# One transfer instead of two for the broadcast rows of a state-space scan

## The chip, the cores and the metric

The kernel runs on one core of a Trainium2 chip. The metric is device time in microseconds (us) of one launch. The core's engines run instruction streams of their own, each strictly in order, and meet only at semaphores: TensorE (PE, matrix products and transposes), VectorE (DVE, among others the scan), ScalarE (ACT, activation functions), GpSimd (POOL, elementwise products here) and SyncE (SP), which does nothing but issue transfers (DMAs) between DRAM and SBUF, the on-chip memory.

## The reference

The input is x of shape 32 x 512 x 256: 32 batches of 512 tokens of 256 features. Each batch goes through a modulated layer norm, causal attention of 16 heads beside a selective state-space layer, a feed-forward layer, and a routed low-rank layer. What the change touches is the state-space recurrence, with 512 inner channels and 16 states n for each:

```python
def step(h, inp):
    xt, dtt, Bt, Ct = inp
    h = jnp.exp(dtt[..., None] * A) * h + (xt * dtt)[..., None] * Bt[:, None, :]
    y = jnp.einsum('bn,bdn->bd', Ct, h)
    return (h, y)
```

B and C are, for each batch, 16 rows of 512 tokens each. They are the same for all channels. Everything is float32 here.

## The kernel before

The 512 channels lie on 128 partitions in four blocks. A scan is one channel block and one state n over all 512 tokens, so a batch has 64 scans, e = 0 to 63. Two scans (two channel blocks, the same n) make a unit, k = 0 to 31, with k = e // 2. A unit goes through these steps:

- SP broadcasts row n of B and row n of C from DRAM (`bc_d`) to all 128 partitions, each into its half of slot k mod 4 of the tile `bc` (function `bc_row`, steps rb_k and rc_k of SP's order, line 438).
- POOL writes the scan inputs of both scans, u times B's row, into two of the eight places of the ring `state` (`fill_states`, step fill_k, L584). It waits for B's row and for the PE sums that last read these two places, of the scans 2k-8 and 2k-7.
- ACT writes the decays into one of two PSUM banks (step dec_e, L708).
- DVE scans (step scan_e, L1201).
- The state is multiplied by C's row: on DVE (step c_e, L1209), or, in every fourth unit (k mod 4 = 3), on POOL (step pc_e, L571). This is the first reader of C's row.
- PE adds the product to the output sums in PSUM (step add_e, L940, four transposing matmuls).

B's half of a slot is free when fill_(k-4) is done (semaphore `b_ok`). C's half is free when the last product of unit k-4 is done, scan 2k-7 (`p_ok` for DVE, `pp_ok` for POOL). SP waits for that before it issues the transfer, and all that stands behind it in SP's order waits as well. Each half of each slot has a semaphore of its own for the landing.

What every engine does in which order is written out by hand in the table `ORDER`, one string for each engine, one turn for each batch. The names of a turn are played again for the next batch; "+" in front means the next batch and "-" the batch before. The turns of batches 2 to 29 are a loop of two turns. Between the scan steps stand the steps of the other layers: in SP's order `xr` (the input again for the residual, and gates, L504 to L510), `put` (the output, L513), `mt` (the row of maxima of the attention, L494), `ld` (q and k for the attention, L481 to L488), `qk` (q and k to DRAM, L458). In SP's order the rc steps do not stand in the order of k: rc11 stands behind rc12, rc13, rc14 and xr; rc19 behind rc20, rc21 and put; rc9 behind rc10; rc6 behind rc8; rc29 behind rc30. The matching rb steps stand far earlier.

## Time and profile before

| | us |
|---|---|
| median of 3 runs | 5942.51 |
| lowest, highest | 5938.76, 5949.41 |
| profiled execution, span | 5938.9 |
| PE busy | 5262.0 (89%) |
| DVE busy | 5103.3 (86%) |
| POOL busy | 4194.8 (71%) |
| ACT busy | 4094.7 (69%) |

The profiled execution is one run; its own time is given by its span, from the first to the last instruction, and it lies within the times of the runs. A share of busy time is a mean over stages that have different limits, so the question at each place is which wait ends last there. "SPq" is SP's queue of issues; the time from an issue to its landing is given apart. The unit of the batch and the number of the scan are not in the trace; they follow from the count of the instructions of a line in the order of the table. The rows below are of two successive batches, called batch 16 and batch 17 by this count (the first is batch 0).

### The profile page before, as it was taken

To read this page: it belongs to the slowest core of one execution; us is meant where nothing else is said; L and a number is where in the kernel's file an instruction comes from. 1 tells how busy PE (TensorE), PEld (TensorE's weight loads), DVE (VectorE), ACT (ScalarE), POOL (GpSimd) and SP (SyncE) were. 2 spreads that over 40 slices of the span, in tenths; PEclk is the share of its full clock that TensorE was granted. 3 is DMA by queue.
4 is the path that set the end of the run, shared out by engine and by line. 5 is a ranking of instruction groups with operands and counts; after the bars stand their busy time and mean duration, and the time that the engine had idled before them with its cause. 6 is when DMAs were issued, how large, how long until landed. Compare 5 with 4: busy or idle time off the path is not lost. (4 is left out here: it accounts for less than half of the span.)

```text
span 5938.9 us, 115651 instructions
## 1 busy us (share of the span) xinstructions
PE 5262.0 (89%) x32280; PEld 3518.1 (59%) x32280; DVE 5103.3 (86%) x7776; ACT 4094.7 (69%) x6407; POOL 4194.8 (71%) x2545
## 2 busy tenths in 40 slices
PE   4799989989898898989989899898988989899986
PEld 2466655656565566656566556565655666565664
DVE  3898889888899898998989898898998989989983
ACT  3677767767776766767767777677767667677763
POOL 3678767767677677776777677676776777767772
PEclk7899999999999999999999999999999999999997
DMA  4444444444454444454444444444444444444441
GB/s 129 132 140 142 140 148 149 142 128 142 135 152 147 129 142 128 144 152 135 143 126 140 144 151 143 127 141 133 152 148 126 142 133 143 151 142 137 142 129 39
DMA packets 521726, 814.74 MB, mean 137 GB/s; under 512 B 80432, under 2 KB 227288, under 8 KB 520976
## 3 DMA queue, kind: packets, MB, share of 16 engines
q1 hardware_dynamic: 513072, 805.79, 44.4%
q8 instruction: 296, 4.85, 0.3%
q14 instruction: 454, 3.72, 0.2%
q10 hardware_dynamic: 7904, 0.39, 0.1%
HBM read 716.50 MB, written 88.38 MB: 136 GB/s over the span
## 5 line engine op out<-in xcount | busy, mean ns | idle before, releaser
L584 POOL TENSOR_TENSOR state<-scan_in,bc 128x1024 f32<-128x1024 f32 x1024 | 2405.9, 2362 | 650.6 <-PE pY L940 504.2
L1201 DVE TENSOR_TENSOR_SCAN pD<-pD,state 128x512 f32<-128x512 f32 x1536 | 1851.2, 1216 | 190.1 <-ACT pD L708 119.9
L708 ACT ACTIVATE pD<-scan_in,A 128x512 f32<-128x512 f32 x2048 | 1397.5, 690 | 656.5 <-DVE state L1209 572.6
L940 PE MATMUL pY<-ident,state 128*128 128x128 f32 x8192 | 1214.0, 282 | 102.9 <-DVE state L1209 94.8
L940 PEld LDWEIGHTS pY<-ident,state 128*128 128x128 f32 x8192 | 928.6, 145 | 335.7 <-DVE state L1209 145.8
L1209 DVE TENSOR_TENSOR state<-pD,bc 128x512 f32<-128x512 f32 x1536 | 1024.6, 680 | 44.7 <-issue 24.6
L1259 DVE TENSOR_REDUCE mx<-pM 128x1 f32<-128x512 f32 (+3 forms) x1408 | 850.3, 630 | 69.8 <-PE pM L1030 67.5
L809 ACT ACTIVATE region<-pM 128x512 f32<-128x512 f32 (+1 forms) x1408 | 733.6, 556 | 255.3 <-PE pM L1048 224.8
L571 POOL TENSOR_TENSOR state<-state,bc 128x512 f32<-128x512 f32 x512 | 644.2, 1273 | 342.9 <-DVE state L1201 333.4
L1201 DVE TENSOR_TENSOR_SCAN state<-pD,state 128x512 f32<-128x512 f32 x512 | 606.0, 1207 | 105.0 <-ACT pD L708 105.0
L1046 PE MATMUL pM<-region 98*128 98x512 bf16 (+3 forms) x2048 | 535.5, 310 | 101.5 <-DMA region<-mrow 45.0
L1028 PE MATMUL pM<-region 96*128 96x512 bf16 (+3 forms) x2048 | 544.8, 314 | 79.2 <-DVE mx L1259 66.8
L1082 PE MATMUL pM<-region,w_f 128*128 128x512 f32 x1024 | 460.1, 600 | 18.1 <-ACT scan_in L846 14.2
L1091 PE MATMUL pM<-w_f,scan_in 128*128 128x256 f32 x2048 | 458.5, 383 | 5.7 <-ACT scan_in L850 5.7
L1091 PEld LDWEIGHTS pM<-w_f,scan_in 128*128 128x128 f32 x2048 | 387.9, 192 | 61.7 <-ACT scan_in L850 10.8
L1030 PE MATMUL pM<-mask_qk,identb 128*128 128x128 bf16 x2048 | 402.1, 225 | 0.0
L962 PE MATMUL pM<-region,vt 128*17 128x512 f32 (+3 forms) x4096 | 359.2, 439 | 46.2 <-ACT region L809 21.1
L1048 PE MATMUL pM<-identb,mask_qk 128*128 128x128 bf16 x2048 | 399.2, 223 | 0.0
L1046 PEld LDWEIGHTS pM<-region 98*128 98x128 bf16 x2048 | 204.1, 101 | 328.6 <-ACT region L809 143.0
L1015 PE MATMUL pM<-w_in,xnT 128*128 128x512 f32 x512 | 277.0, 668 | 96.0 <-issue 67.0
L1082 PEld LDWEIGHTS pM<-region,w_f 128*128 128x128 f32 x1024 | 189.5, 191 | 248.1 <-issue 210.5
L1028 PEld LDWEIGHTS pM<-region 96*128 96x128 bf16 x2048 | 205.8, 101 | 215.3 <-DVE mx L1259 121.0
(171 smaller groups left out, 8360.6 us busy)
## 6 DMA issues: line engine op xcount, KB each, us to landing
bc<-bc_d SPq DMA_DIRECT2D x2048, 256.0 KB, 4.0
region<-qk_d SPq DMA_DIRECT2D x640, 128.0 KB, 3.6
qk_d<-qkp SPq DMA_DIRECT2D x64, 384.0 KB, 2.6
qk_d<-ht SPq DMA_DIRECT2D x64, 384.0 KB, 3.1
xt<-in_x_dram SPq DMA_DIRECT2D x32, 512.0 KB, 5.7
hres_d<-xt SPq DMA_DIRECT2D x32, 512.0 KB, 5.1
region<-qk_d SPq DMA_DIRECT2D x256, 64.0 KB, 3.0
x<-hres_d SPq DMA_DIRECT2D x32, 512.0 KB, 5.9
```

What stands on the lines that cost most here:

```text
L571: nc.gpsimd.tensor_tensor(slot, slot, bc[:, e // JP % BC_SLOTS, 1, :], ALU.mult).then_inc(pp_ok.sem, 1)
L584: nc.gpsimd.tensor_tensor(state[:, at_:at_ + JP], us[:, parity(b), k // N * JP:(k // N + 1) * JP, :], bc[:, k % BC_SLOTS, 0, :].unsqueeze( ...
L708: act.activation(pD[DECAY_BANK[e]][:], dts[:, parity(b), j], ACT.Exp, scale=A[:, j, n:n + 1]).then_inc(a_ok.sem, 1)
L809: act.activation(probs[kb % 2][:, h:h + heads, 0:n], pM[bank_of(name)][:, 0:heads * n].rearrange("p (h t) -> p h t", h=heads), ACT.Exp, sc ...
L940: ins = pe.matmul(y_part(t, e % JP), state[:, e % RING, t * P:(t + 1) * P], ident[:], is_transpose=True, start=False, stop=(e % PASS >= PA ...
L1028: pe.matmul(ps[:, s * n:(s + 1) * n], q[0:QK_ROWS, h, qb * P:(qb + 1) * P], kk[0:QK_ROWS, h, 0:n], start=True, stop=False, skip_group_chec ...
L1046: pe.matmul(ps[:, i * n:(i + 1) * n], kk[0:QK_ROWS + 2, h + i, kb * P:(kb + 1) * P], q[0:QK_ROWS + 2, h + i, kb * P:L], start=True, stop=F ...
L1082: ins = pe.matmul(ps[:], w_f1[:, k, f * P:(f + 1) * P], h2T[:, k], start=(k == 0), stop=(k == KT - 1))
L1091: ins = pe.matmul(ps[:, t * D:(t + 1) * D], gT(b)[:, f, (2 * n + t) * P:(2 * n + t + 1) * P], w_f2[:, f, :], start=(f == 0), stop=(f == FT ...
L1201: v.tensor_tensor_scan(h if e in POOL_C else decay, decay, h, 0.0, ALU.mult, ALU.add)\
L1209: v.tensor_tensor(state[:, e % RING], pD[DECAY_BANK[e]][:], bc[:, slot, 1, :], ALU.mult)\
L1259: v.tensor_reduce(mx[:, g % 2].rearrange("p (h q) -> p h q", q=TB)[:, heads[0]:heads[-1] + 1, qb], pM[bank_of(name)][:, 0:len(heads) * n]. ...
```

## The change

B's and C's rows of a unit come with one transfer of 512 KB into both halves of the slot, with one semaphore. It is issued where C's row was issued, behind the wait for the last product of unit k-4. The rb steps go from SP's order; nothing else in any order is moved. POOL's fill and POOL's and DVE's products wait for the same semaphore.

```diff
--- before.py
+++ after.py
@@ -314,7 +314,7 @@
         dt_ps, dt_x, dt_e, dt_ok, u_ok = (sig("dt_ps", J), sig("dt_x", 2 * J), sig("dt_e", 2),
                                           sig("dt_ok", 1), sig("u_ok", 2))
         xd_ok, d_done = sig("xd_ok", J), sig("d_done", PASSES)
-        bc_in = [[sem(f"{row}_in{s}") for s in range(BC_SLOTS)] for row in "bc"]
+        bc_in = [sem(f"bc_in{s}") for s in range(BC_SLOTS)]
         a_ok, b_ok, s_ok, p_ok, y_ok = (sig("a_ok", SCANS), sig("b_ok", SCANS), sig("s_ok", SCANS),
                                         sig("p_ok", len(DVE_C)), sig("y_ok", SCANS))
         pp_ok = sig("pp_ok", len(POOL_C))
@@ -424,23 +424,19 @@
                 sp.dma_start(Ks[s][QK_ROWS:QK_ROWS + 2], ones_d).then_inc(ones_in, 16)
             sp.dma_start(mod_cols.rearrange("b p c -> p b c"), mod_t).then_inc(cols_stored, 16)
 
-            def bc_row(b, k, row):
+            def bc_rows(b, k):
 
                 slot = k % BC_SLOTS
 
                 before, last = (b, k - BC_SLOTS) if k >= BC_SLOTS else (b.next(-1), k - BC_SLOTS + UNITS)
                 if before.reg is not None or before.off >= 0:
-                    e = JP * last + JP - 1
-                    if row == 0:
-                        before.wait(sp, b_ok, e + 1)
-                    else:
-                        before.wait(sp, *product_after(e))
-                sp.dma_start(bc[:, slot, row], bc_d[b.index, k // N, row * N + k % N].partition_broadcast(P))\
-                  .then_inc(bc_in[row][slot], 16)
+                    before.wait(sp, *product_after(JP * last + JP - 1))
+                sp.dma_start(bc[:, slot], bc_d[b.index, k // N].rearrange("(r n) t -> n r t", r=2)[k % N]
+                             .partition_broadcast(P)).then_inc(bc_in[slot], 16)
 
             def step(name, b):
-                if name[:2] in ("rb", "rc"):
-                    bc_row(b, int(name[2:]), int(name[1] == "c"))
+                if name[:2] == "rc":
+                    bc_rows(b, int(name[2:]))
                 elif name == "load" and b.reg is None and b.off == 0:
                     pass
                 elif name == "load":
@@ -559,15 +555,15 @@
             def row(ap):
                 return ap.unsqueeze(1).broadcast_to([P, TB, D])
 
-            def row_in(b, k, row):
-
-                return Signal(bc_in[row][k % BC_SLOTS], 16 * UNITS // BC_SLOTS), 16 * (k // BC_SLOTS + 1)
+            def rows_in(b, k):
+
+                return Signal(bc_in[k % BC_SLOTS], 16 * UNITS // BC_SLOTS), 16 * (k // BC_SLOTS + 1)
 
             def times_c(b, e):
 
                 slot = state[:, e % RING]
                 b.wait(pool, s_ok, e + 1)
-                b.wait(pool, *row_in(b, e // JP, 1))
+                b.wait(pool, *rows_in(b, e // JP))
                 nc.gpsimd.tensor_tensor(slot, slot, bc[:, e // JP % BC_SLOTS, 1, :], ALU.mult).then_inc(pp_ok.sem, 1)
 
             def fill_states(b, k):
@@ -575,7 +571,7 @@
                 e, at_ = k * JP, k * JP % RING
                 if k == 0:
                     b.wait(pool, u_ok)
-                b.wait(pool, *row_in(b, k, 0))
+                b.wait(pool, *rows_in(b, k))
 
                 if e >= RING:
                     b.wait(pool, y_ok, e + JP - RING)
@@ -1205,7 +1201,7 @@
 
                 slot = e // JP % BC_SLOTS
                 b.wait(dve, s_ok, e + 1)
-                b.wait(dve, Signal(bc_in[1][slot], 16 * UNITS // BC_SLOTS), 16 * (e // JP // BC_SLOTS + 1))
+                b.wait(dve, Signal(bc_in[slot], 16 * UNITS // BC_SLOTS), 16 * (e // JP // BC_SLOTS + 1))
                 v.tensor_tensor(state[:, e % RING], pD[DECAY_BANK[e]][:], bc[:, slot, 1, :], ALU.mult)\
                  .then_inc(p_ok.sem, 1)
 
@@ -1362,10 +1358,9 @@
 
 ORDER = {engine: parse(text) for engine, text in {
     "SP": """
-        -rb22 -rb25 -rb23 -ld3 -rc23 -rb24 -mt2 -rc25 -rb26 -rc24 -rb27 -x1p -rc26 -rc28 -rb28 -rb29 -rc27 xp
-        -rb30 ld0 -mt3 -rb31 -rc30 -rc29 -rc31 +load rb1 rb0 rc0 rc1 rc2 rb2 rb3 rc3 rb4 ld2 rc4 rb5 rc5 rb7 rb6
-        rb8 rb9 rc8 rc6 rc7 ld1 rb10 rc10 rc9 rb11 rb12 rc12 rb13 rc13 rc14 -xr rc11 rc15 mt0 rb15 rc16 rb16 rb14
-        +qk0 +qk1 rb18 rc17 +qk2 rb20 rb17 rc18 +l1a rb19 mt1 rc20 rb21 +qk3 rc21 -put rc19 rc22
+        -ld3 -rc23 -mt2 -rc25 -rc24 -x1p -rc26 -rc28 -rc27 xp ld0 -mt3 -rc30 -rc29 -rc31 +load rc0 rc1 rc2 rc3 ld2
+        rc4 rc5 rc8 rc6 rc7 ld1 rc10 rc9 rc12 rc13 rc14 -xr rc11 rc15 mt0 rc16 +qk0 +qk1 rc17 +qk2 rc18 +l1a mt1
+        rc20 +qk3 rc21 -put rc19 rc22
     """,
     "POOL": """
         fill8 fill9 pc14 -f1_0 pc15 +l0s fill10 +l0a fill11 +l0b +l0c +l1s fill12 pc22 pc23 fill13 -x2 -x2b -l3s
```

What stands in SP's order at two places, and in POOL's at one. "bc<-bc_d" is the broadcast; p_ok and pp_ok are products done on DVE and POOL, b_ok is a fill done. First, SP's order before, from rb10 to the first transfer of mt0 of a batch, with xr (the rows from in_x_dram to mod_cols) in it:

```order
L438 DMA bc<-bc_d 128x512 [waits b_ok]
L438 DMA bc<-bc_d 128x512 [waits p_ok] x2
L438 DMA bc<-bc_d 128x512 [waits b_ok] x2
L438 DMA bc<-bc_d 128x512 [waits p_ok]
L438 DMA bc<-bc_d 128x512 [waits b_ok]
L438 DMA bc<-bc_d 128x512 [waits p_ok] x2
L504 DMA region<-in_x_dram 128x4x256 [waits so_ps,built]
L506 DMA region<-mod_rows 128x256 x3
L510 DMA mod_f<-mod_cols 128x4 [waits cols_stored]
L438 DMA bc<-bc_d 128x512 [waits pp_ok] x2
L494 DMA region<-mrow 1x16x128 [waits mr_ok]
```

The same stretch of SP's order in the changed kernel:

```order
L434 DMA bc<-bc_d 128x2x512 [waits p_ok] x5
L500 DMA region<-in_x_dram 128x4x256 [waits so_ps,built]
L502 DMA region<-mod_rows 128x256 x3
L506 DMA mod_f<-mod_cols 128x4 [waits cols_stored]
L434 DMA bc<-bc_d 128x2x512 [waits pp_ok] x2
L490 DMA region<-mrow 1x16x128 [waits mr_ok]
```

The rows with b_ok (rb10 to rb13) are gone, and the five broadcasts ahead of xr are rc10, rc9, rc12, rc13 and rc14. The first row with pp_ok behind mod_f is rc11 in both: the transfer for unit 11 is still issued behind the one that waits for the products of unit 10, but it now carries B's row as well.

Second, SP's order before, from rc20 on, with qk3 and put (out_dram) in it:

```order
L438 DMA bc<-bc_d 128x512 [waits p_ok]
L438 DMA bc<-bc_d 128x512 [waits b_ok]
L458 DMA qk_d<-ht 128x3x512 [waits qk_lo]
L438 DMA bc<-bc_d 128x512 [waits p_ok]
L513 DMA out_dram<-scan_in 128x4x256 [waits o_fin]
L438 DMA bc<-bc_d 128x512 [waits pp_ok]
L438 DMA bc<-bc_d 128x512 [waits p_ok]
```

And in the changed kernel:

```order
L434 DMA bc<-bc_d 128x2x512 [waits p_ok]
L454 DMA qk_d<-ht 128x3x512 [waits qk_lo]
L434 DMA bc<-bc_d 128x2x512 [waits p_ok]
L509 DMA out_dram<-scan_in 128x4x256 [waits o_fin]
L434 DMA bc<-bc_d 128x2x512 [waits pp_ok]
L434 DMA bc<-bc_d 128x2x512 [waits p_ok]
```

The row behind out_dram is rc19 in both: B's row of unit 19, which had come far earlier, now comes there.

Third, POOL's order around the fill of unit 11 (the second row of L584, or of L580), before:

```order
L584 TENSOR_TENSOR state<-scan_in,bc 128x1024 [waits y_ok,b_in2]
L600 TENSOR_TENSOR ht<-xt,mod_a 128x1024 [waits qk_out1,moda_in,n0]
L584 TENSOR_TENSOR state<-scan_in,bc 128x1024 [waits y_ok,b_in3]
L603 TENSOR_TENSOR ht<-ht,mod_a 128x1024 [waits h_made]
L606 TENSOR_TENSOR xt<-ht,ob_row 128x1024 [waits h_made]
L551 TENSOR_TENSOR ln_rs<-ln_mv,eps 128x4 [waits mv1]
```

And in the changed kernel, where lines are four lower:

```order
L580 TENSOR_TENSOR state<-scan_in,bc 128x1024 [waits y_ok,bc_in2]
L596 TENSOR_TENSOR ht<-xt,mod_a 128x1024 [waits qk_out1,moda_in,n0]
L580 TENSOR_TENSOR state<-scan_in,bc 128x1024 [waits y_ok,bc_in3]
L599 TENSOR_TENSOR ht<-ht,mod_a 128x1024 [waits h_made]
L602 TENSOR_TENSOR xt<-ht,ob_row 128x1024 [waits h_made]
L547 TENSOR_TENSOR ln_rs<-ln_mv,eps 128x4 [waits mv1]
```

No instruction moves on POOL. What a fill waits for is bc_in, the landing of both rows, in place of b_in, the landing of B's row.

## Rows read from the trace of the kernel before

**Rows 1.** Windows of batch 16 to 17: stretch, its length, busy us, clock, DMA, GB/s.
```profile
3064.00:3149.00 85.00, 76.08 (x546) 48.09 (x545) 82.90 (x124) 58.52 (x94) 58.52 (x31) 0.96 0.54 163
3156.00:3208.00 52.00, 51.75 (x271) 36.42 (x270) 51.17 (x77) 38.10 (x59) 44.41 (x30) 1.00 0.54 160
...
3028.00:3063.00 35.00, 30.19 (x145) 21.58 (x146) 18.08 (x38) 23.43 (x36) 22.32 (x19) 0.95 0.23 78
```

**Rows 2.** The tile state, whole run: instructions (ns), then idle time by releaser.
```profile
L584 POOL TENSOR_TENSOR state<-scan_in,bc x1024: 2338/2362/2392, 120.7 to 5826.6; 128x1024 f32<-128x1024 f32 x171
...
  DMA bc<-bc_d: 135.0, 57
  POOL state L584: 65.9, 22
```

**Rows 3.** Page, DMA queue (packets, MB, share) and issues (count, KB, us to landing).
```profile
q1 hardware_dynamic: 513072, 805.79, 44.4%
...
bc<-bc_d SPq DMA_DIRECT2D x2048, 256.0 KB, 4.0
...
x<-hres_d SPq DMA_DIRECT2D x32, 512.0 KB, 5.9
```

**Rows 4.** Tile bc on SP, window 3092.84 to 3093.3: rc19 of batch 16.
```profile
L438 SPq DMA_DIRECT2D bc<-bc_d x1: 492/492/492, 3092.8 to 3092.8; - x1
...
DMA to landing us min/median/max: 6.3/6.3/6.3
```

**Rows 5.** Timelines (start, duration us) of POOL and DVE: fill19 and scan38, batch 16.
```profile
3092.12 2.37 POOL L584 TENSOR_TENSOR state<-scan_in,bc 128x1024 f32<-128x1024 f32 x1
...
3095.02 1.20 DVE L1201 TENSOR_TENSOR_SCAN state<-pD,state 128x512 f32<-128x512 f32 x1
```

**Rows 6.** Timelines of batch 17: rc9, fill9, fill10, scan20.
```profile
3188.61 0.59 SPq L438 DMA_DIRECT2D bc<-bc_d  x1
...
3188.74 2.35 POOL L584 TENSOR_TENSOR state<-scan_in,bc 128x1024 f32<-128x1024 f32 x1
...
3197.59 2.36 POOL L584 TENSOR_TENSOR state<-scan_in,bc 128x1024 f32<-128x1024 f32 x1
...
3199.99 1.23 DVE L1201 TENSOR_TENSOR_SCAN pD<-pD,state 128x512 f32<-128x512 f32 x1
```

**Rows 7.** Timelines of batch 17: rc14, rc11, fill11, fill12, scan22, scan24.
```profile
3204.12 0.33 SPq L438 DMA_DIRECT2D bc<-bc_d  x1
...
3207.42 0.33 SPq L438 DMA_DIRECT2D bc<-bc_d  x1
...
3204.60 2.37 POOL L584 TENSOR_TENSOR state<-scan_in,bc 128x1024 f32<-128x1024 f32 x1 [1.27 <-PE pY L940]
...
3213.32 2.36 POOL L584 TENSOR_TENSOR state<-scan_in,bc 128x1024 f32<-128x1024 f32 x1
...
3207.10 1.21 DVE L1201 TENSOR_TENSOR_SCAN state<-pD,state 128x512 f32<-128x512 f32 x1
...
3215.71 1.23 DVE L1201 TENSOR_TENSOR_SCAN pD<-pD,state 128x512 f32<-128x512 f32 x1 [3.11 <-POOL state L584]
```

**Rows 8.** Timeline of DVE, batch 16: scan23 and scan26.
```profile
3037.51 1.22 DVE L1201 TENSOR_TENSOR_SCAN state<-pD,state 128x512 f32<-128x512 f32 x1 [6.55 <-ACT pD L708]
...
3046.78 1.23 DVE L1201 TENSOR_TENSOR_SCAN pD<-pD,state 128x512 f32<-128x512 f32 x1 [3.59 <-ACT pD L708]
```

**Rows 9.** Timelines of batch 16: rc29, fill29, scan58.
```profile
3140.06 0.33 SPq L438 DMA_DIRECT2D bc<-bc_d  x1
...
3141.42 2.37 POOL L584 TENSOR_TENSOR state<-scan_in,bc 128x1024 f32<-128x1024 f32 x1 [0.41 <-PE pY L940]
...
3143.88 1.22 DVE L1201 TENSOR_TENSOR_SCAN pD<-pD,state 128x512 f32<-128x512 f32 x1
```

**Rows 10.** Timelines of batch 17: rc6, fill6, scan12.
```profile
3178.78 0.33 SPq L438 DMA_DIRECT2D bc<-bc_d  x1
...
3179.82 2.37 POOL L584 TENSOR_TENSOR state<-scan_in,bc 128x1024 f32<-128x1024 f32 x1 [2.36 <-PE pY L940]
...
3184.06 1.22 DVE L1201 TENSOR_TENSOR_SCAN pD<-pD,state 128x512 f32<-128x512 f32 x1
```

## The prediction, made before the changed kernel was run

> **What bounds the kernel now.** I read the windows first. Over 85 us of batch 16 DVE is busy for 82.90 us, and over the 52 us from 3156 for 51.17 us [rows 1]. PE is full there too, but DVE's order of scans and products sets the pace: what comes late on DVE in these stretches is not given back, because no idle time is there to give it. Only the 35 us from 3028 differ: DVE is busy for 18.08 us of them [rows 1], since its scans there wait for ACT [rows 8]. Next I read the tile `state`. POOL made its 1024 fills between 120.7 and 5826.6 us, so a batch of 32 takes 5706 / 32 = 178 us and a unit 5.6 us. POOL sat idle 135.0 us for a broadcast row (57 times), but DVE sat idle for a fill only 65.9 us in the whole run [rows 2]. So the fills run just ahead of the scans, and this is the margin that the change spends. Last I read single fills with the transfer and the scan that belong to them [rows 4 to 10]: the issue on SP, the start on POOL, and the start of the scan that reads the fill.
>
> **What is removed.** 1024 of 2048 issues on SP, and 1024 waits of SP for fills. SP computes nothing, and C's rows were awaited by products that come after the scan, so the removal gains time only where a transfer was awaited. At most that is the 65.9 us in which DVE waited for a fill [rows 2]. I take nothing, and keep 0 to -66 us.
>
> **What is added: a longer transfer.** The main queue's transfers kept 16 engines busy for 44.4% of 5938.9 us, 2637 us for 805.79 MB [rows 3]. That is 0.86 us for 256 KB (0.262 MB). A broadcast of 256 KB lands 4.0 us after its issue, one of x of 512 KB after 5.9 us [rows 3]. For the new one I take 4.0 + 0.9 = 4.9 us, with 4.0 and 5.9 us as the ends: the long one has the same 2 KB rows as the short one, so it should cost its bytes alone.
>
> The Trainium skill (SBUF — State Buffer, "The DMA setup-cost knee") says that every transfer pays about 2 us whatever its size, plus bytes at 436 GB/s, and that one should coalesce; by that, 512 KB would land after 3.2 us. The trace's 4.0 us for 256 KB lies above that line already (2.6 us by it). With 3.2 us the five transfers of the sum below would each land 1.7 us earlier, 8.5 us for a batch, near 6300 us. DMA: Bandwidth & Descriptors ("Rules for kernel authors") says to issue early and wait late; that speaks against this change, whatever the size of a transfer.
>
> **What is moved: B's row, from early to late.** A fill could start as soon as POOL and the ring were free. Now it also waits for the transfer that stood at C's place. For each place: new landing = old issue of C's row + 4.9; new start of the fill = that landing, if later than before; delay of DVE = new end of the fill (2.37 us long) - old start of its scan. The four places where that is positive and not covered:
>
> 1. Unit 19. Its transfer stands behind put on SP. It was issued at 3092.8 and landed 6.3 us later in that crowd [rows 4], so the new one lands at 3092.8 + 6.3 + 0.9 = 3100.0. fill19 started at 3092.12 and now ends at 3102.4; its scan started at 3095.02 [rows 5]. Delay 7.4 us. If the crowd is thinner, the median of 4.9 us in place of 7.2 gives 5.1. I take 6.3. DVE is full behind it, so it stays.
>
> 2. Units 9 and 11, batch 17. rc9, behind rc10, was issued at 3188.61: landing 3193.5, fill9 4.8 us after its old 3188.74. POOL's work from fill9 to fill10 is without a gap, so fill10 moves from 3197.59 to 3202.4 and ends at 3204.8, where scan20 had started at 3199.99 [rows 6]: 4.8 us. The products of unit 10 move with it, so rc14, which waits for them (3204.12), moves to 3208.9. xr follows (five issues, 3.3 us from rc14 to rc11), rc11 goes from 3207.42 to 3212.2 and lands at 3217.1, where fill11 had started at 3204.60. That is 12.5 us. Queued behind fill11 on POOL are two products of the layer norm, the statistics, fill12, two products with C and fill13; DVE's layer norm statistics and scan24, released by fill12, wait for them. scan22 had 0.1 us to spare (3207.10 against fill11's end at 3206.97), and scan24 had already idled 3.11 us for fill12 [rows 7]. So 12.5 us.
>
> 3. Units 9 and 11, batch 16. The lateness is the same, but here scan23 idled 6.55 us and scan26 3.59 us for ACT [rows 8], waits that come through PE and ACT, and not through a broadcast. They cover 6.55 us surely and the 3.59 us partly: between 2.4 and 6.0 us are left. I take 4. Batches of the loop's first and second turn alternate, so the mean of both is 8.2 us, with 6 and 11 as the ends.
>
> 4. Unit 29. rc29 was issued at 3140.06: landing 3145.0, where fill29 had started at 3141.42; it ends at 3147.3, and scan58 had started at 3143.88 [rows 9]. 3.4 us.
>
> 5. Unit 6. rc6 stands behind rc8 and was issued at 3178.78: landing 3183.7, where fill6 had started at 3179.82; it ends at 3186.1, and scan12 had started at 3184.06 [rows 10]. 2.0 us.
>
> The other units get nothing: either their C's row landed long before the fill, or (units 23 to 27) POOL is ahead of the scans by more than the lateness. What is left of the latter, and unit 4, I hold at 0 to 4 us for a batch.
>
> **The sum.** 6.3 + 8.2 + 3.4 + 2.0 = 19.9 us for a batch. Of 32 batches 31 have both neighbours: 31 x 19.9 = 617 us. The profiled execution's span of 5938.9 us plus 617 is 6556 us. The median of the runs (5942.51) is 3.6 us above that span, so I predict 6560 us, 10% slower.
>
> **The rivals.**
>
> A. The delays are covered. PE is the busiest engine over the run, and the attention's steps between the scans wait for each other. If each delay shortens a later wait on DVE as in batch 16, a half goes: 10 us for a batch, 6250 us. For it speaks the 35 us stretch in which DVE is half idle [rows 1, 8]; against it that three of the places (units 19, 29 and 6) have DVE at 97% or more behind them.
>
> B. The delays feed each other. A late product makes the next issue on SP late, and all in SP's queue behind it (q and k, the maxima) with it; units 23 to 27 begin to count, and the transfers land after 5.9 us. That adds 1 us at five places and 4 us at the others: 29 us for a batch, 6840 us. Unit 11 already shows such a chain inside the sum.
>
> C. Faster: one transfer for two, at SP's queue. The mechanism is that the queue empties earlier, since rb steps no longer block it behind fills, so that rows land before fills ask for them. Price: at most the 65.9 us of DVE's waits for fills, 5876 us. It decides only if C's old issue plus 4.9 us comes ahead of the fill at nearly every unit. The rows of five units say otherwise, by 3.6 to 12.5 us [rows 4 to 10].
>
> D. The one transfer behaves as two (512 KB in two halves with one semaphore, landing after 5.9 us or more), and so the change does less for the queue than it says. That is the upper end of the transfer's cost: 1 us more for five transfers of a batch, 6710 us. It is within my range.
>
> E. No change: every late fill finds a scan with as much to spare. It needs more than 3 us of margin at units 6, 9, 11, 19 and 29, where the rows show 0 to 1.9 us [rows 5 to 7, 9, 10].
>
> **How the numbers follow.** My case, the delays pass DVE at these places (D included): 0.74, its own range 6350 to 6800: with a landing of 4.0 us five transfers give back 4.5 us, with 5.9 us they add 5.0, and units 9 and 11 lie between 6 and 11 us, so 13.2 to 27.7 us for a batch. A: 0.12. B: 0.08. C: 0.03. E: 0.03. A range that leaves 2 in 10 out: 6340 to 6810. What a measurement of this kernel can tell from no change is about 0.2%, 12 us. Faster by more: 0.03; within: 0.03; slower: 0.94.
>
> **What the changed profile would show.** POOL's idle time for the DMA of bc grows from 135 us to well over 1000, and DVE's idle time for POOL's fills from 66 us to 400 or more. The 512 KB broadcast lands in 4.9 us at the median. The longest waits of a batch for a broadcast are fill19 (some 7 us) and fill11 (7 to 8 us after POOL is free), and the wait of fill11 begins after the products of unit 10. SP's waits for b_ok are gone. DVE's and PE's busy times stay within 1%; a batch takes 198 us and not 178. I am wrong if fill11 or fill19 starts without a wait for a DMA, if the landing is under 4 us, or if DVE's idle time grows by much less than the 20 us for a batch that I add up.

## The result and the profile after

The changed kernel takes 7217.99 us (median of 4 runs, 7214.77 to 7227.56), against 5942.22 us for the kernel before (median of 4 runs), measured with it. The ratio is 1.215 with a 95% interval of 1.2133 to 1.2167: 21.5% slower, a loss of 1275 us. Slower was forecast, but 10% and a loss of 617 us, with 6340 to 6810 us as the range. The sign and the named places were right. One place was missing from the forecast, unit 24, and the size was half of what came.

The page of the changed kernel; its lines are numbered 4 lower than those of the kernel before, so that fills are L580 (L584), POOL's products with C L567 (L571), scans L1197 (L1201), DVE's products with C L1205 (L1209) and the maxima L1255 (L1259). Columns of the first lines: busy us, share of the span, instructions.

```profile
span 7214.1 us, 111939 instructions
...
PE 5575.4 (77%) x32280; PEld 3707.9 (51%) x32280; DVE 5126.4 (71%) x7776; ACT 4112.2 (57%) x6407; POOL 4184.0 (58%) x2545
...
PEclk7889989889888989889899888898888898898887
...
q1 hardware_dynamic: 496688, 805.72, 40.5%
...
bc<-bc_d SPq DMA_DIRECT2D x1024, 512.0 KB, 5.7
...
x<-hres_d SPq DMA_DIRECT2D x32, 512.0 KB, 9.6
```

DVE is busy for 5126.4 us, 0.5% more than before (5103.3), and the bytes are the same [rows 3]. So all but 23 of the 1275 us are idle time on DVE, not work. The new transfer lands after 5.7 us at the median, where I took 4.9. The load of x, whose own bytes did not change, lands after 9.6 us and not 5.9 [rows 3]. PE's busy time rose by 313 us (5262.0 to 5575.4) at the same 32280 instructions; the digits of its clock, nearly all 9 before, are 8 and 9 now.

The tile `state` over the whole run, as in [rows 2]: the fills (ns), then POOL's idle time by what ended it (us, times).

```profile
L580 POOL TENSOR_TENSOR state<-scan_in,bc x1024: 2330/2354/2402, 120.7 to 7097.1; 128x1024 f32<-128x1024 f32 x171
...
  DMA bc<-bc_d: 1545.9, 228
```

And the waits of the changed kernel (total us, times, the longest):

```profile
POOL state L580 <- DMA bc<-bc_d: 1545.9, 228, 14.5
...
DVE pD L1197 <- POOL state L580: 578.1, 209, 7.2
DVE state L1197 <- POOL state L580: 570.5, 65, 11.6
...
DVE mx L1255 <- PE pM L1026: 266.4, 247, 17.3
...
PE pY L936 <- POOL state L567: 251.7, 38, 8.5
```

POOL waited 135.0 us for broadcast rows before [rows 2], and waits 1545.9 us now. DVE waited 65.9 us for fills [rows 2], and waits 578.1 + 570.5 = 1148.6 us now. Two of the rows are ones that the forecast had not looked for: DVE's maxima of the attention wait 266.4 us for PE (67.5 us before), and PE waits 251.7 us for POOL's product with C.

**Where the time goes within a batch.** DVE runs the same 7776 instructions in the same order in both kernels, so their starts can be set against each other one by one. The table, called the ledger below, shows what each place adds to the distance from scan18 of a batch to scan18 of the next, in us, as a mean over batches 4 to 27, even and odd ones apart (even ones are the loop's first turn). Units 0 to 8 in a column belong to the batch that follows, so the even column's units 4 and 6 are those of odd batches.

| place | even | odd | mean | forecast |
|---|---|---|---|---|
| units 9 and 11, net of what later waits give back | 5.9 | 16.6 | 11.3 | 8.2 |
| unit 19 (scan38) | 7.65 | 7.5 | 7.6 | 6.3 |
| maxima behind unit 24 (mx3_4 to mx3_6) | 5.6 | 5.8 | 5.7 | 0 |
| unit 24 (scan48) | 3.9 | 3.8 | 3.85 | 0 |
| unit 29 (scan58) | 3.75 | 3.6 | 3.7 | 3.4 |
| unit 6 (scan12) | 2.7 | 1.7 | 2.2 | 2.0 |
| unit 4 (scan8, scan10) | 2.0 | 0 | 1.0 | 0 |
| xs2, a wait for ACT | 0.9 | 1.2 | 1.05 | 0 |
| further waits for ACT (scan5, scan15, scan61, a maximum), less what scan60 gives back | 1.8 | 3.9 | 2.8 | 0 |
| sum | 34.2 | 44.1 | 39.2 | 19.9 |

31 x 39.2 = 1215 of the 1275 us; the other 60 lie outside the batches of the mean, and I did not place them. Single places follow, all of batch 14, an even one.

**Unit 19.** SP's issue and POOL's and DVE's timelines (start, duration, and in brackets the idle time before and what ended it):

```profile
3306.11 0.42 SPq L434 DMA_DIRECT2D bc<-bc_d  x1
...
3313.70 2.34 POOL L580 TENSOR_TENSOR state<-scan_in,bc 128x1024 f32<-128x1024 f32 x1 [8.23 <-issue]
...
3316.07 1.22 DVE L1197 TENSOR_TENSOR_SCAN state<-pD,state 128x512 f32<-128x512 f32 x1 [7.66 <-POOL state L580]
```

The transfer was issued at 3306.11. The tile bc on SP in the window of this issue:

```profile
DMA to landing us min/median/max: 7.5/7.5/7.5
```

It lands 7.5 us later, 0.3 more than worked out for the crowd (6.3 before, [rows 4], plus 0.9), at about 3313.6, and the fill starts at 3313.70. The bracket on POOL names "issue" and not the DMA, although the landing and the start stand next to each other: a releaser is inferred, and where it doesn't fit, the times decide. DVE idles for 7.66 us where before scan38 followed with no wait [rows 5].

**Units 9 and 11.** The same views, first fill9 and scan20, then rc14 and rc11, fill11, and scan22, scan23 and scan24:

```profile
3218.22 2.35 POOL L580 TENSOR_TENSOR state<-scan_in,bc 128x1024 f32<-128x1024 f32 x1 [4.35 <-DMA bc<-bc_d]
...
3229.35 1.23 DVE L1197 TENSOR_TENSOR_SCAN pD<-pD,state 128x512 f32<-128x512 f32 x1 [2.95 <-POOL state L580]
...
3233.33 0.37 SPq L434 DMA_DIRECT2D bc<-bc_d  x1
...
3238.00 0.38 SPq L434 DMA_DIRECT2D bc<-bc_d  x1
...
3244.53 2.35 POOL L580 TENSOR_TENSOR state<-scan_in,bc 128x1024 f32<-128x1024 f32 x1 [12.81 <-DMA bc<-bc_d]
...
3246.91 1.22 DVE L1197 TENSOR_TENSOR_SCAN state<-pD,state 128x512 f32<-128x512 f32 x1 [10.55 <-POOL state L580]
...
3250.96 1.19 DVE L1197 TENSOR_TENSOR_SCAN state<-pD,state 128x512 f32<-128x512 f32 x1
...
3255.59 1.23 DVE L1197 TENSOR_TENSOR_SCAN pD<-pD,state 128x512 f32<-128x512 f32 x1 [3.44 <-POOL state L580]
```

The chain runs as forecast: fill9 waits for its transfer, scan20 idles 2.95 us, rc14 waits for the products of unit 10, xr follows, rc11 is issued at 3238.00 and lands 6.4 us later, and DVE idles 10.55 us at scan22. Two sizes differ: from rc14 to rc11 it takes 4.7 us and not 3.3 [rows 7], and the landing 6.4 and not 4.9. At scan23 the wait for ACT of 6.55 us [rows 8] is gone: it is the cover that the forecast counted on in even batches.

**Unit 24, which the forecast held at nothing.** SP's queue in the changed kernel stands `rc23 mt2 rc25 rc24 x1p rc26`. SP's rows of batch 14, then POOL, PE and DVE behind them:

```profile
3335.50 1.18 SPq L490 DMA_DIRECT2D region<-mrow  x2
...
3336.93 1.00 SPq L434 DMA_DIRECT2D bc<-bc_d  x2
...
3338.26 0.37 SPq L495 DMA_DIRECT2D x<-hres_d  x1
...
3346.08 6.95 POOL L580 TENSOR_TENSOR state<-scan_in,bc 128x1024 f32<-128x1024 f32 x3 [10.70 <-DMA bc<-bc_d]
...
3352.99 1.26 POOL L567 TENSOR_TENSOR state<-state,bc 128x512 f32<-128x512 f32 x1
...
3354.30 1.12 PE L936 MATMUL pY<-ident,state 128*128 128x128 f32 x4 [7.05 <-POOL state L567]
...
3355.64 0.53 PE L1024 MATMUL pM<-region 96*128 96x384 bf16 x1
...
3348.46 2.35 DVE L1197 TENSOR_TENSOR_SCAN pD<-pD,state 128x512 f32<-128x512 f32 x2 [3.20 <-POOL state L580]
...
3356.31 0.56 DVE L1255 TENSOR_REDUCE mx<-pM 128x1 f32<-128x384 f32 x1 [4.33 <-PE pM L1026]
```

rc24 is the second of the two issues at 3336.93. It is in flight with three more transfers of 512 KB, all issued within 2 us: rc25 ahead of it, x's load (3338.26) and rc26 (3338.87) behind. It lands after 8.3 us. fill24 has waited 10.70 us by then, and scan48 idles 3.20 us for it. That is one delay. The second comes from POOL's queue: fill24, fill25 and fill26 stand ahead of pc46, the product with C of scan46, which was ready. pc46 starts at 3352.99, PE has idled 7.05 us for it, the attention's matmul behind it comes late, and DVE's maximum idles 4.33 us. One late transfer costs twice, at the scan of its own unit and at work of another kind that is queued behind its fill.

### The profile page after: what moved, and what is told of

The parts are those of the page before. It is cut to its first block and busy times, and to the rows that moved or that the text cites. A ratio compares the mean times of both kernels' runs of the same rounds, so it can differ in the third digit from the quotient of the medians.

```text
span 7214.1 us, 111939 instructions
## 1 busy us (share of the span) xinstructions
PE 5575.4 (77%) x32280; PEld 3707.9 (51%) x32280; DVE 5126.4 (71%) x7776; ACT 4112.2 (57%) x6407; POOL 4184.0 (58%) x2545
## 3 DMA queue, kind: packets, MB, share of 16 engines
q1 hardware_dynamic: 496688, 805.72, 40.5%
## 5 line engine op out<-in xcount | busy, mean ns | idle before, releaser
L580 POOL TENSOR_TENSOR state<-scan_in,bc 128x1024 f32<-128x1024 f32 x1024 | 2400.7, 2355 | 2193.4 <-DMA bc<-bc_d 1545.9
L1197 DVE TENSOR_TENSOR_SCAN pD<-pD,state 128x512 f32<-128x512 f32 x1536 | 1854.2, 1218 | 699.9 <-POOL state L580 578.1
L936 PE MATMUL pY<-ident,state 128*128 128x128 f32 x8192 | 1305.2, 297 | 356.2 <-POOL state L567 251.7
L936 PEld LDWEIGHTS pY<-ident,state 128*128 128x128 f32 x8192 | 1011.3, 154 | 645.3 <-POOL state L567 269.8
L1205 DVE TENSOR_TENSOR state<-pD,bc 128x512 f32<-128x512 f32 x1536 | 1024.5, 680 | 45.2 <-issue 25.1
L1197 DVE TENSOR_TENSOR_SCAN state<-pD,state 128x512 f32<-128x512 f32 x512 | 608.3, 1208 | 608.8 <-POOL state L580 570.5
L1255 DVE TENSOR_REDUCE mx<-pM 128x1 f32<-128x512 f32 (+3 forms) x1408 | 850.3, 630 | 267.4 <-PE pM L1026 266.4
L1024 PE MATMUL pM<-region 96*128 96x512 bf16 (+3 forms) x2048 | 585.7, 333 | 253.6 <-DVE mx L1255 211.4
L567 POOL TENSOR_TENSOR state<-state,bc 128x512 f32<-128x512 f32 x512 | 642.7, 1272 | 235.3 <-DVE state L1197 235.3
L1042 PE MATMUL pM<-region 98*128 98x512 bf16 (+3 forms) x2048 | 570.6, 328 | 67.0 <-DMA region<-mrow 41.4
L958 PE MATMUL pM<-region,vt 128*17 128x512 f32 (+3 forms) x4096 | 401.0, 489 | 259.3 <-ACT region L805 245.7
L1087 PE MATMUL pM<-w_f,scan_in 128*128 128x256 f32 x2048 | 487.6, 400 | 5.7 <-ACT scan_in L846 5.7
L1087 PEld LDWEIGHTS pM<-w_f,scan_in 128*128 128x128 f32 x2048 | 411.6, 204 | 66.5 <-ACT scan_in L846 6.5
L1011 PE MATMUL pM<-w_in,xnT 128*128 128x512 f32 x512 | 298.2, 712 | 177.6 <-issue 92.0
L1044 PE MATMUL pM<-identb,mask_qk 128*128 128x128 bf16 x2048 | 418.9, 234 | 0.0
L1237 DVE SCALAR_TENSOR_TENSOR xc<-pM,conv_w,xc 128x511 f32<-128x511 f32 (+2 forms) x384 | 286.4, 746 | 47.2 <-ACT xc L764 36.9
```

The source lines that it names most:

```text
L567: nc.gpsimd.tensor_tensor(slot, slot, bc[:, e // JP % BC_SLOTS, 1, :], ALU.mult).then_inc(pp_ok.sem, 1)
L580: nc.gpsimd.tensor_tensor(state[:, at_:at_ + JP], us[:, parity(b), k // N * JP:(k // N + 1) * JP, :], bc[:, k % BC_SLOTS, 0, :].unsqueeze( ...
L936: ins = pe.matmul(y_part(t, e % JP), state[:, e % RING, t * P:(t + 1) * P], ident[:], is_transpose=True, start=False, stop=(e % PASS >= PA ...
L1024: pe.matmul(ps[:, s * n:(s + 1) * n], q[0:QK_ROWS, h, qb * P:(qb + 1) * P], kk[0:QK_ROWS, h, 0:n], start=True, stop=False, skip_group_chec ...
L1042: pe.matmul(ps[:, i * n:(i + 1) * n], kk[0:QK_ROWS + 2, h + i, kb * P:(kb + 1) * P], q[0:QK_ROWS + 2, h + i, kb * P:L], start=True, stop=F ...
L1087: ins = pe.matmul(ps[:, t * D:(t + 1) * D], gT(b)[:, f, (2 * n + t) * P:(2 * n + t + 1) * P], w_f2[:, f, :], start=(f == 0), stop=(f == FT ...
```

## The experiments

The names in the quoted expectations: theory P, of the place, says that the loss comes from B's row being issued and awaited where C's row was; theory S, of the size (and S2, a form of it), says that it comes from the transfer of 512 KB itself. All ratios are to the kernel before, measured with each group of experiments: 5947.22 us for experiments 1 to 4, 5945.35 for 5 to 8, 5945.19 for 9 to 12. The changed kernel was measured beside 5942.22 us alone, so a difference from it carries these few us of spread as well.

**1. B's row late, as two transfers (late_b).** The kernel before, with its two transfers of 256 KB and two semaphores, but B's row issued right ahead of C's, at C's place:

```diff
-        -rb22 -rb25 -rb23 -ld3 -rc23 -rb24 -mt2 -rc25 -rb26 -rc24 -rb27 -x1p -rc26 -rc28 -rb28 -rb29 -rc27 xp
+        -ld3 -rb23 -rc23 -mt2 -rb25 -rc25 -rb24 -rc24 -x1p -rb26 -rc26 -rb28 -rc28 -rb27 -rc27 xp ld0 -mt3 -rb30 -rc30
...
```

> Two transfers of 256 KB on two semaphores as in the kernel before, but B's row is issued right ahead of C's, at C's place. Theory P (the loss is that B's row comes at C's place, behind the product of four units back and behind what stands there in SP's order): nearly all of the loss stays. Against the changed kernel B's row lands about 1 us earlier (first of two), at some six places of a batch, so 7218 - 6 x 31 x 1 = about 7030 to 7200 us. Theory S (one large transfer in one piece, with its longer landing, makes the loss): most of the 1276 us comes back, under 6500 us.

Measured: 6789.7 us, ratio 1.1422 (1.1403 to 1.1442). That is 843 of the 1271 us by which the changed kernel stands above the 5947.22 us of the kernel before. The place is the larger part, but not all, so the result lies between the two expectations. The ledger against the kernel before gives 20.6 us for an even batch and 31.1 for an odd one: 8.2 and 7.8 at scan22, 7.2 and 6.4 at scan38, 4.4 at mx3_4 in both, 2.6 and 2.5 at scan58, but only 1.2 and 1.4 at scan48. DVE's idle time for fills, tile `state` of this kernel:

```profile
  POOL state L584: 782.2, 236
```

**2 to 4. One step of SP's table moved in the changed kernel.** m24 puts rc24 ahead of mt2, m11 puts rc11 ahead of rc12, m19 puts rc19 ahead of rc20. The first, as an example:

```diff
-        -ld3 -rc23 -mt2 -rc25 -rc24 -x1p -rc26 -rc28 -rc27 xp ...
+        -ld3 -rc23 -rc24 -mt2 -rc25 -x1p -rc26 -rc28 -rc27 xp ...
```

> The changed kernel with one step moved in SP's order: the transfer for unit 24 goes from behind mt2 and the one for unit 25 to ahead of mt2. By the ledger of DVE's delays, unit 24 costs 3.9 us a batch at its scan and 5.6 us at the attention's maxima just behind, which wait for PE. Theory P with the chain (late fill 24 to 26, so late products with C on POOL for unit 23, so PE stands at add46, so the maxima are late): both go, 31 x 9.5 = 295 us, about 6920 us. Rival: the maxima wait for PE for another reason (the lower TensorE clock, q and k landing late): only 31 x 3.9 = 120 us, about 7100 us.

> The changed kernel with one step moved in SP's order: the transfer for unit 11 goes from behind the one for unit 14 and xr to ahead of the one for unit 12. Theory P: fill11 no longer waits for the products of unit 10 and five issues. DVE's wait of 10.5 us before scan22 goes; in batches of even number 7 us of it were covered by a later wait, in odd ones none: (3 + 11) / 2 x 31 = 220 us less, about 7000 us. Rival (POOL is late anyway because of fill9 and fill10): under 100 us less.

> The changed kernel with one step moved in SP's order: the transfer for unit 19 goes from behind put to ahead of the one for unit 20. Theory P: DVE's wait of 7.6 us before scan38 goes and is not given back elsewhere: 31 x 7.6 = 235 us less, about 6980 us. Rival (DVE runs into the next wait, for PE or for the fill of unit 24): under 100 us less.

Measured: m24 7051.0 us (1.1859, 1.1839 to 1.1879), 167 us less than the changed kernel; m11 6978.66 us (1.1737, 1.1718 to 1.1757), 239 less; m19 6998.67 us (1.1762, 1.1742 to 1.1781), 219 less. The last two came out as expected, to about 20 us. m24 came out between its two expectations of 6920 and 7100 us; its runs spread from 7021 to 7057 us, and the profiled one is the fastest. Each transfer's place is a cause by itself. At m24 the delay of scan48 is gone, but the maximum still waits; DVE's and POOL's timelines of this kernel (batch 13):

```profile
3049.08 2.34 DVE L1197 TENSOR_TENSOR_SCAN pD<-pD,state 128x512 f32<-128x512 f32 x2
...
3056.01 0.56 DVE L1255 TENSOR_REDUCE mx<-pM 128x1 f32<-128x384 f32 x1 [3.42 <-PE pM L1026]
...
3050.38 2.35 POOL L580 TENSOR_TENSOR state<-scan_in,bc 128x1024 f32<-128x1024 f32 x1 [1.38 <-DMA bc<-bc_d]
3052.69 2.48 POOL L567 TENSOR_TENSOR state<-state,bc 128x512 f32<-128x512 f32 x2
```

scan48 has no bracket now, and mx3_4 idles 3.42 us. The ledger gives 2.3 us less at mx3_4 in even and 0.9 in odd batches, of 4.4. The POOL rows show what still holds it: fill26, whose transfer comes behind x1p, waits 1.38 us for that transfer, and pc46 follows right behind it. pc46 now starts 7.0 us after scan46 in the median, 12.4 in the changed kernel and 2.7 before.

**5. Two transfers on the one semaphore (pair_sem).** The changed kernel with each unit's rows as two transfers of 256 KB, with the waits unchanged, on both:

```diff
-                sp.dma_start(bc[:, slot], bc_d[b.index, k // N].rearrange("(r n) t -> n r t", r=2)[k % N]
-                             .partition_broadcast(P)).then_inc(bc_in[slot], 16)
+                for r in range(2):
+                    sp.dma_start(bc[:, slot, r], bc_d[b.index, k // N, r * N + k % N].partition_broadcast(P))\
+                      .then_inc(bc_in[slot], 16)
...
-                return Signal(bc_in[k % BC_SLOTS], 16 * UNITS // BC_SLOTS), 16 * (k // BC_SLOTS + 1)
+                return Signal(bc_in[k % BC_SLOTS], 32 * UNITS // BC_SLOTS), 32 * (k // BC_SLOTS + 1)
```

> The changed kernel, but B's and C's rows come with two transfers of 256 KB, one right behind the other, at the same place and on the one shared semaphore. Theory S2 (one large transfer alone keeps only half of the 16 engines busy at a time, where two in flight together fill them, so the 512 KB land late): the pair lands about 1 us earlier than the one, so near the kernel with B's row right ahead of C's on semaphores of its own (6790 us), 6800 to 6900 us. Rival (the shared semaphore makes the loss, since a fill now waits for C's row too): no gain, 7150 to 7220 us.

Measured: 7136.86 us (1.2012, 1.1992 to 1.2032), 81 us less than the changed kernel. From late_b it differs in that the two rows are tied together: there a fill waits for B's row only, and SP issues that row once the fill that last read its half is done; here the fill waits for both rows, and both wait for the products. The tie costs 7137 - 6790 = 347 us, and that the two are one transfer costs 81. The expectation of 6800 to 6900 was wrong; it had put the rest of late_b down to the size of the transfer. The 1271 us are thus 843 for the place, 347 for the tie and 81 for the one transfer, in this order of SP's table; experiment 12 shows that the shares depend on it. Its page gives the time to landing of each half:

```profile
bc<-bc_d SPq DMA_DIRECT2D x2048, 256.0 KB, 4.6
```

The 4.6 us are the median of both halves. The first lands after 4.1 us; the second is issued 0.5 us behind it and lands after 4.9. The pair is complete 5.4 us after its first issue, the one of 512 KB after 5.7; at unit 24 it is 7.0 against 8.8, and the ledger gives 2.5 us at scan48 and not 3.85. The Trainium skill (Perfetto Trace Analysis, "DMA Optimizations") says that splitting a transfer may let the task finish sooner where the DMA engines are mostly idle; they are at 40.5% here, and the 81 us agree with it.

**6. The same bytes in pieces of 4 KB (rows4k).** B's and C's rows of a unit lie side by side in HBM, so that the transfer reads 4 KB in one piece for each partition, not two of 2 KB (writing the rows to HBM takes two transfers more for a batch):

```diff
-        bc_d = dram("bc_d", (B, PASSES, 2 * N, L))
+        bc_d = dram("bc_d", (B, PASSES, N, 2, L))
...
+                sp.dma_start(bc[:, slot].rearrange("p r t -> p (r t)"),
+                             bc_d[b.index, k // N, k % N].rearrange("r t -> (r t)").partition_broadcast(P)).then_inc(bc_in[slot], 16)
...
```

> The changed kernel with B's and C's row of a state next to each other in DRAM, so that the one transfer of 512 KB is made of 128 pieces of 4 KB and not of 256 of 2 KB (the rows are written with two transfers more for each half of the batch). If the number of pieces sets the landing of a lone transfer (256 pieces went out at some 72 a us), it falls from 5.7 to about 4 us and the time to about 6800 us. If the bytes set it, the landing stays and the time is 7200 us.

Measured: 6909.61 us (1.1622, 1.1602 to 1.1641), 308 us less, between the two expectations. Queue and issues on its page, then POOL and DVE at unit 24 of batch 14:

```profile
q1 hardware_dynamic: 366640, 805.73, 36.6%
...
bc<-bc_d SPq DMA_DIRECT2D x1024, 512.0 KB, 4.5
...
3216.10 6.97 POOL L582 TENSOR_TENSOR state<-scan_in,bc 128x1024 f32<-128x1024 f32 x3 [9.88 <-DMA bc<-bc_d]
...
3218.48 2.35 DVE L1199 TENSOR_TENSOR_SCAN pD<-pD,state 128x512 f32<-128x512 f32 x2
...
3226.34 0.56 DVE L1257 TENSOR_REDUCE mx<-pM 128x1 f32<-128x384 f32 x1 [4.35 <-PE pM L1028]
```

The bytes are the same; there are 130048 packets fewer (366640 for 496688), and the landing comes after 4.5 us, not 5.7. So "it should cost its bytes alone" was wrong for the transfer as the change makes it, and near right for one with longer pieces: the step from 4.0 to 4.5 us is less than the 0.86 us of its bytes. At unit 24, with SP's order unchanged, the transfer lands after 5.0 us and not 8.8. scan48 is late by 0.1 (even) to 0.3 us (odd) in the ledger and not 3.85, but the maxima behind it still lose 5.6 us: the first delay hangs on the landing, the second on POOL's queue. The same section of the Trainium skill says that going from 2 KB to 4 KB for a DMA can help much; the runs agree if that is read of the piece, since the whole transfer was 512 KB both times. The 3.2 us that the setup-cost rule gives for 512 KB, cited in the prediction, are reached by neither layout (least landings 3.8 and 3.3 us).

**7. POOL's products ahead of the late fills (pc_first).** In the changed kernel:

```diff
-        pc39 fill22 fill23 fill24 fill25 fill26 pc46 pc47 fill27 fill28 pc54 pc55 fill29 fill30 fill31 +u0 +u1
+        pc39 fill22 fill23 pc46 pc47 fill24 fill25 fill26 fill27 fill28 pc54 pc55 fill29 fill30 fill31 +u0 +u1
```

> The changed kernel with POOL's two products of unit 23 ahead of its fills 24 to 26, not behind them; SP's order as in the changed kernel. Chain theory (fill24 late, then fill25, fill26, the products of unit 23, then PE at add46, then the attention's maxima and DVE): DVE's wait of 5.6 us for the maxima behind scan49 goes, 31 x 5.6 = 170 us, about 7045 us. Rival (PE is late there for another reason): 7180 to 7230 us.

Measured: 7073.12 us (1.1908, 1.1889 to 1.1928), 145 us less, near the expected 170. DVE's timeline of this kernel, scan48 and mx3_4 of batch 13:

```profile
3075.19 2.35 DVE L1197 TENSOR_TENSOR_SCAN pD<-pD,state 128x512 f32<-128x512 f32 x2 [3.35 <-POOL state L580]
...
3078.62 0.55 DVE L1255 TENSOR_REDUCE mx<-pM 128x1 f32<-128x384 f32 x1
```

The wait for fill24 is there still (3.35 us), the maximum's wait is gone. The chain over POOL's queue and PE to DVE is shown: the ledger gives 5.0 us for a batch at the maxima, more than 145 / 31 = 4.7.

**8. All transfers in the order of the units (sorted).** The changed kernel with SP's table put in order. rc9, rc19, rc24 and others stand ahead of the rows of later units again, and with that rc11 ahead of xr, rc19 ahead of put and rc24 ahead of mt2:

```diff
-        ... rc5 rc8 rc6 rc7 ld1 rc10 rc9 rc12 rc13 rc14 -xr rc11 rc15 ... mt1 rc20 +qk3 rc21 -put rc19 rc22
+        ... rc5 rc6 rc7 rc8 ld1 rc9 rc10 rc11 rc12 rc13 rc14 -xr rc15 ... mt1 rc19 rc20 +qk3 rc21 -put rc22
```

> The changed kernel with the transfers in SP's order put in the order of the units (6 and 7 ahead of 8, 9 ahead of 10, 11 ahead of 12, 19 ahead of 20, 24 ahead of mt2 and 25, 27 ahead of 28, 29 ahead of 30). Theory P: the single moves gave 167, 239 and 219 us (24, 11, 19); units 6, 9 and 29 add about 2 + 3 + 3.6 us a batch, 250 us together: 7218 - 875 = 6340 us. Rival (POOL's fills are late anyway by the landing of 5.7 us behind the product of four units back): the moves do not add up, above 6600 us.

Measured: 6276.78 us (1.0552, 1.0535 to 1.057), 941 us less, where 6340 was expected. Of a loss of 1271 us, three quarters hang on a table that had been made for C's rows, which are first read after the scan. The tile `state` and scan38 (batch 15) of this kernel:

```profile
  POOL state L580: 251.3, 173
```

```profile
3071.72 1.22 DVE L1197 TENSOR_TENSOR_SCAN state<-pD,state 128x512 f32<-128x512 f32 x1 [1.71 <-POOL state L580]
```

DVE's idle time for fills falls from 1148.6 to 251.3 us, and scan38 idles 1.71 us and not 7.66. The ledger against the kernel before is 11.4 and 9.7 us for a batch.

**9 and 10. The order and the pieces together (sorted4k), and with POOL's products first as well (sorted4k_pc).** No new edits, only those of 6, 7 and 8 joined.

> One transfer for both rows, made of 128 pieces of 4 KB, with the transfers in the order of the units. The order alone leaves 332 us of the loss (6277 us), the pieces alone took 308 us off the changed kernel. What is left in the ordered kernel are six places where the landing behind the product of four units back is late by about 2 us each; 1.2 us less at each is 6 x 1.2 x 31 = 220 us: about 6055 us. If the two do not add (the fills then wait for PE's sums, as before the change): 6100 us or more.

> As the one before, with POOL's products of unit 23 ahead of its fills 24 to 26. In the ordered kernel DVE still waits 2.0 to 2.7 us a batch for the maxima behind scan49; the chain theory takes up to 2.4 x 31 = 74 us off: about 5980 us. Rival: the fills 24 to 26 are on time there, so nothing is gained, or the products wait for scan47 and hold up fill24: 0 to +30 us.

Measured: 6098.55 us (1.0257, 1.0239 to 1.0275) and 6177.78 us (1.0385, 1.0364 to 1.0407). The first is what was expected if the two do not add (6100). The pieces of 4 KB bring 178 us here and brought 308 in the order of the change: with fewer fills late, a shorter landing is worth less. POOL's products first cost 79 us here, though they had gained 145 in the changed kernel; the rival had named such a cost, but of 30 us at most.

**11. A control: the kernel before with the same move on POOL (base_pc).** The edit of experiment 7.

> The kernel before the change with the same move on POOL alone (products of unit 23 ahead of fills 24 to 26). DVE waits nowhere for it there, so no change within 0.2%, 5930 to 5955 us. It is the control for the move.

Measured: 6059.12 us (1.0191, 1.0174 to 1.0208), 114 us more than before, where no change was expected. POOL's timeline of pc46 and fill24, and DVE's scan48 (batch 16):

```profile
3178.51 1.26 POOL L571 TENSOR_TENSOR state<-state,bc 128x512 f32<-128x512 f32 x1 [10.49 <-DVE state L1201]
...
3181.45 2.35 POOL L584 TENSOR_TENSOR state<-scan_in,bc 128x1024 f32<-128x1024 f32 x1
...
3183.83 1.23 DVE L1201 TENSOR_TENSOR_SCAN pD<-pD,state 128x512 f32<-128x512 f32 x1 [2.52 <-POOL state L584]
```

When the transfers are in time, POOL runs ahead of DVE. Then pc46 waits 10.49 us for its scan, and fill24 waits behind it until DVE runs dry for 2.52 us. POOL's place of pc46 is right while fills are early, and wrong only once they are late. Experiment 10 shows the same: its pc46 waits 9.35 us for scan46 and its scan48 2.51 us for fill24 (batch 14), and the ledger gives 2.6 us at scan48 for both kernels. So a gain from that move can't be counted as a part of the change's loss that adds to the others.

**12. The order of the units, with two transfers and two semaphores (late_b_sorted).**

```diff
-        -rb22 -rb25 -rb23 -ld3 -rc23 -rb24 -mt2 -rc25 -rb26 -rc24 -rb27 -x1p -rc26 -rc28 -rb28 -rb29 -rc27 xp
+        -ld3 -rb23 -rc23 -rb24 -rc24 -mt2 -rb25 -rc25 -x1p -rb26 -rc26 -rb27 -rc27 -rb28 -rc28 xp ld0 -mt3 -rb29 -rc29
...
```

> Two transfers on two semaphores, B's row right ahead of C's, in the order of the units. Place alone, without the joint landing: in the unordered kernel the joint semaphore and transfer cost 428 us (6790 against 7218). If that is the same share of the ordered kernel's loss (a third), 6165 us; if the landing matters at each of the six places by 1.4 us, 6277 - 260 = 6015 us.

Measured: 6077.25 us (1.0212, 1.0188 to 1.0236), between the two expectations. It is 200 us below sorted, with the same places and two transfers, and 21 us below sorted4k. The tie and the one transfer together cost 428 us in the change's order and 200 in this one; the place alone costs 843 us in the one and 132 in the other. None of the twelve beats the kernel before: the early B row has a value that no order tried here gave back. More buffers for the rows, which would let them be issued earlier, were not tried.

## Why the prediction was right in sign and wrong in size

*What bounds the kernel.* Right. DVE's busy time is the same to 0.5%, and most delays of DVE stay in the span. "DVE's and PE's busy times stay within 1%" held for DVE and failed for PE (6% more).

*What is removed.* Right to take nothing. SP's free queue brought no gain that any row shows.

*The longer transfer.* Mis-sized: 4.9 us forecast, 5.7 measured at the median. Two pieces of 2 KB for each partition cost more than their bytes: with one of 4 KB the landing is 4.5 us, and this step from 5.7 to 4.5 is worth 308 us in the change's order and 178 in the sorted one. The upper end of 5.9 us did hold the median, and of the rivals D named it, but it was priced at five places for 1 us each, 155 us. And a median is the wrong figure for a transfer issued among others: over batches 4 to 27 the landing was 6.3 to 6.4 us at units 6, 11 and 29, 7.4 at unit 19 and 8.8 at unit 24.

*Unit 19.* 6.3 us forecast, 7.6 measured. I had worked out 7.4 from the crowd on the queue and then taken 1.1 off in case the crowd were thinner. The rows read 7.5 us to landing; nothing in the trace stood behind the discount. m19 showed 219 us for this place, against 7.6 x 31 = 236 by the ledger.

*Units 9 and 11.* 8.2 us as a mean forecast, 11.3 measured: 5.9 for 4 in even batches and 16.6 for 12.5 in odd ones. The mechanism was right to the step (rc14 behind the products of unit 10, xr, rc11). The row of unit 11 comes later than taken, by its landing and by xr's issues ahead of it, and odd batches have nothing to cover that. The cover in even batches came as forecast: 7.3 us at scan23 and some at scan26. m11 gave 239 us.

*Units 29 and 6.* 3.4 and 2.0 us forecast, 3.7 and 2.2 measured. Right in size, in part by luck: both transfers landed after 6.3 us or more and not 4.9, but against the scan before they were issued earlier than in the old kernel, by 0.9 us at unit 29 and 1.3 to 1.5 at unit 6, and the two nearly cancel.

*The step that failed:* "The other units get nothing: either their C's row landed long before the fill, or (units 23 to 27) POOL is ahead of the scans by more than the lateness." Unit 24 cost 3.85 us at its scan and the maxima behind it 5.7 us: 9.6 x 31 = 296 us, almost half of the 658 that were missing. It failed in two ways.

First, POOL's lead was not more than the lateness, by the forecast's own rule. These are rc24, fill24 and scan48 of batch 16 in the kernel before, which I did not show:

```profile
3116.06 0.33 SPq L438 DMA_DIRECT2D bc<-bc_d  x1
...
3110.56 2.34 POOL L584 TENSOR_TENSOR state<-scan_in,bc 128x1024 f32<-128x1024 f32 x1 [0.70 <-DMA bc<-bc_d]
...
3123.09 1.22 DVE L1201 TENSOR_TENSOR_SCAN pD<-pD,state 128x512 f32<-128x512 f32 x1
```

With 4.9 us the transfer lands at 3120.96, 10.4 us after the old start of the fill, which then ends at 3123.33, 0.24 us after the old start of the scan. The whole lead is spent, and any longer landing shows on DVE. It was 8.8 us, with three other transfers of 512 KB issued within 2 us of this one, a crowd that I had priced at unit 19 only. The issue itself was not late: 3.6 us ahead of scan46, where it had been 3.0 before. The delay of scan48 follows the landing, at the same place in SP's order: 3.85 us with 8.8, 2.5 with 7.0 (pair_sem), 0.1 to 0.3 with 5.0 (rows4k).

Second, I had weighed POOL's lead over the scans and left out what else stands in POOL's queue: pc46, for which PE and then DVE's maxima wait, stood behind three fills. That needs no late scan; in rows4k the scan is in time and the maxima still lose 5.6 us. pc_first took the maxima's wait away and left the scan's; m24 took the scan's and a part of the maxima's. The two moves were not run together in the change's order.

*The rest.* Of the 19.3 us for a batch that were missing, 9.6 belong to unit 24 and its chain, 3.1 to units 9 and 11, 1.3 to unit 19, 1.0 to unit 4, 0.5 to units 29 and 6, 3.9 to waits for ACT that grew behind these (xs2 and others). The last I did not test one by one. Unit 4 was in reach of the same rule: in batch 17 of the kernel before, rc4 was issued at 3168.14 and scan8 started at 3173.59, which gives 1.8 us, against 2.0 measured for such batches.

*The rivals.* B, "the delays feed each other" with units 23 to 27 in it, at 6840 us and a chance of 0.08, was nearest, in size and in naming units 23 to 27 and a landing near 5.9 us, and even it fell short by 378 us. A was wrong: later waits give much back only in even batches, and new waits come up elsewhere. C, E: nothing speaks for them. The range was too narrow above: its upper end of 27.7 us for a batch is 19.9 + 5.0 + 2.8, the bounds of the known terms alone. The 0 to 4 us that the prediction held for the other units are not in it, and those units cost some 10.6 (unit 24 with its maxima, and unit 4).

*The signs.* Held: POOL's idle time for the DMA well over 1000 us, DVE's for fills over 400, fill11's wait behind the products of unit 10. Missed: the landing, the 7 to 8 us of fill11 (12.81 us in batch 14; 2.9 us of the excess come from the two sizes named above, and 1.3 from counting from fill11's old start, before which POOL had been free for 1.27 us [rows 7]), and the 198 us for a batch: (7097.1 - 120.7) / 32 = 218. A window of 220 us, about one batch long, from batch 14 of the changed kernel (length; busy us of PE, PEld, DVE, ACT, POOL; clock, DMA share, GB/s):

```profile
3212.00:3432.00 220.00, 175.32 (x1021) 116.20 (x1020) 162.54 (x245) 131.59 (x206) 132.50 (x80) 0.91 0.41 118
```

## What to carry to other kernels

Before joining two transfers, ask when each half is first needed and when its buffer comes free. The joined one is issued at the later of the two times and awaited at the earlier of the two needs, and here that cost 1190 us of 1271, while making one transfer of two cost 81. Before calling a buffer's lead large enough, set the lead against the lateness in rows, with the landing of a transfer in that crowd and not the median: unit 24 had 10.2 us of lead for 10.4 us of lateness. For each transfer that comes late, list all that is queued behind the waiting instruction on its engine, not just the consumer of that buffer. Unit 24's late row cost more at an unrelated maximum (5.7 us) than at its own scan (3.85 us). An order tuned for one set of arrival times is to be tuned again when these change (941 us here). And an edit that helps in the late kernel can harm in the timely one (-145 and +114 us).
